# Graph attention with neighbour rows gathered for whole tiles: blocks of edges aligned to tiles instead of to groups of four tiles

## The reference

```python
Wh = x @ W_w + W_b
e = (Wh @ a_w[:256])[col] + (Wh @ a_w[256:])[row] + a_b[0]     # row = src, col = dst
e = where(e > 0, e, 0.2 * e)
m = segment_max(e, row)
ex = exp(e - m[row])
att = ex / segment_sum(ex, row)[row]
h = relu(segment_sum(att[:, None] * Wh[col], row))             # one row of 256 per edge is fetched
```

## Time and profile before

| what | us |
|---|---|
| median of three runs | 2610.23 (2609.86 to 2613.34) |
| profiled execution, its own time | 2611.51 |
| span of its trace | 2609.7 |
| first gather to last `gather_up` begins | 739.0 to 2081.7 |
| busy in the span: PE, PEld | 2045.7, 1599.1 |
| busy in the span: DVE, ACT, POOL | 1908.9, 1587.7, 1356.0 |

### The profile page before, as it was taken

The page is one execution under the profiler, slowest core; times in us unless marked ns, Lnnn a source line. Parts: engine busy times, 40 slices in busy tenths (PEclk is TensorE's granted clock), DMA queues, the critical chain, the costliest instruction groups (busy, mean ns, idle before and its releaser), DMA issues. The chain is left out here.

```text
span 2609.7 us, 49796 instructions
## 1 busy us (share of the span) xinstructions
PE 2045.7 (78%) x10254; PEld 1599.1 (61%) x10254; DVE 1908.9 (73%) x6660; ACT 1587.7 (61%) x4949; POOL 1356.0 (52%) x1284
## 2 busy tenths in 40 slices
PE   2888766788738788888888888888888766099997
PEld 1444355677636666666666666666766556088886
DVE  7877689999857878878888887788888664045453
ACT  4566375333137778878887788778877764033332
POOL 0000000011257777777777777777777447645555
PEclk9999968899869989999999899989989866599999
DMA  4100000111133433333333333333333265435553
GB/s 147 40 27 27 19 10 19 50 24 24 21 83 106 111 106 106 107 106 108 106 106 108 109 105 107 107 108 107 106 107 105 64 180 131 116 69 92 96 93 59
DMA packets 130120, 223.27 MB, mean 86 GB/s; under 512 B 37607, under 2 KB 80660, under 8 KB 129820
## 3 DMA queue, kind: packets, MB, share of 16 engines
q0 software_dynamic: 78864, 160.18, 25.3%
q1 hardware_dynamic: 49418, 58.93, 7.6%
q10 hardware_dynamic: 1538, 1.31, 0.2%
HBM read 171.72 MB, written 49.77 MB: 85 GB/s over the span
## 5 line engine op out<-in xcount | busy, mean ns | idle before, releaser
L1213 POOL DMA_INDIRECT area<-wh_table,area x1004 | 1010.9, 1007 | 319.4 <-issue 299.4
L1453 PE MATMUL bank<-area 128*126 128x258 f32 x2008 | 563.9, 429 | 48.5 <-ACT area L1398 39.1
L1453 PEld LDWEIGHTS bank<-area 128*126 128x126 f32 x2008 | 399.4, 209 | 155.1 <-ACT area L1398 86.7
L512 POOL DMA_INDIRECT sorted_slots<-area x28 | 45.7, 1633 | 672.2 <-issue 486.3
L1398 ACT ACTIVATE area<-area 128x126 f32<-128x126 f32 x1004 | 317.5, 388 | 97.5 <-issue 84.4
L1242 DVE TENSOR_SCALAR area<-iota_row,area 128x126 f32<-128x126 f32 x1004 | 358.7, 361 | 21.1 <-issue 7.5
L1389 ACT ACTIVATE area<-iota_row,area 128x126 f32<-128x126 f32 x1004 | 315.9, 388 | 0.0
L1435 PE MATMUL bank<-ident,area 128*126 128x128 f32 x1004 | 168.4, 294 | 115.6 <-DVE area L1242 114.5
L1943 POOL DMA_INDIRECT out_dram<-area x108 | 169.9, 1573 | 160.3 <-DVE area L2002 143.5
L1435 PEld LDWEIGHTS bank<-ident,area 128*126 128x126 f32 x1004 | 122.6, 147 | 163.1 <-DVE area L1242 129.3
L1472 PE MATMUL bank<-area 128*128 128x250 f32 x800 | 201.1, 395 | 0.0
(11 more groups left out here) (340 smaller groups left out, 4281.0 us busy)
## 6 DMA issues: line engine op xcount, KB each, us to landing
area<-wh_table,area POOLq DMA_INDIRECT x1004
area<-moe_rows SPq DMA_DIRECT2D x54, 264.0 KB, 2.7
wh_table<-area SPq DMA_DIRECT2D x50, 126.0 KB
xn<-in_x_dram SPq DMA_DIRECT2D x25, 250.0 KB
x_rows<-area SPq DMA_DIRECT2D x25, 250.0 KB
area<-x_rows SPq DMA_DIRECT2D x25, 250.0 KB
area<-in_L_ffn_expert_w_dram SPq DMA_DIRECT2D x3, 1536.0 KB, 12.0
out_dram<-xn SPq DMA_DIRECT2D x2, 1500.0 KB
```

Of the source, the lines that this page charges most:

```text
L1213: g.indirect_dma_start(out=gath[:, s % RG, t, :], out_offset=None, in_=table, in_offset=bass.IndirectOffsetOnAxis(ap=idx_tab[:, s * GT + t ...
L1453: last = T.matmul(bank[US][0:RW, 0:WROW], sm[:, b, t, :], gath[:, j % RG, t, :], start=(t == 0), stop=(t == GT - 1))
```

## The change

A node block's edges now begin at a whole tile, not at a whole group. There are TILES = 860 tiles (215 ring blocks of four). NG is still 251: each node block is still cut into groups of four tiles from its own first tile, and the last group of a block reaches into the next block's tiles. The slots of a foreign tile must not count, so `row_tab` now holds row + 2^17 x block, and `shifted` subtracts 2^17 x (the group's block), which gives `rowl`; slots of another block match no row. The 60.0 bound on the exponent (`score_bound`) goes, and the distance factor becomes 1e12.

The gathered tiles lie in a ring of 40 tile places (RS), in the order of tiles. A group's first tile (`tile_tab`), its place in the ring (`slot_tab`), how many tiles it needs (`group_tab` row 0), where its new scores go (`group_tab` row 32) and its block (row 64) are tables in SBUF which the engines load into registers, group by group. SP hands on two counts: `room` to POOL when a ring block has been used up (it loads the group number from `group_tab` row 96 and waits for `p_main` against it), and `ready` to DVE when a ring block has landed.

`own` becomes `own_all` for every block, filled with the row score parts once, so the copy in `group_peak` goes. ACT's `divide` writes the maximum's parts there and loads the block's register. The `x1` reload moves from SP's queue to ACT's. The first stage gains the instructions that make the tables.

```diff
-GS, GS_BITS = GT * L, 9
-NG = (E + NT * (LO - 1 + GS - 1)) // GS
-TILES = NG * GT
+MOST = (E + NT * (LO - 1 + L - 1)) // L
+NG = (MOST + NT * (GT - 1)) // GT
+NB = -(-(MOST + GT - 1) // GT)
+TILES = NB * GT
...
+                for b in range(NB):
+                    f = b + AHEAD
+                    if RING <= f < NB:
+                        sp.reg_load(uses[f % 2], group_tab[96:97, f - RING:f - RING + 1])
+                        sp.wait_ge(p_main, sp.snap(uses[f % 2], min_val=1, max_val=NG))
+                        sp.sem_inc(room, 1)
+                    sp.wait_ge(gathered[b % RING], 16 * GT * (b // RING + 1))
+                    sp.sem_inc(ready, GT)
...
-                for s in range(NG):
-                    if s >= RG:
-                        g.wait_ge(p_main, s - RG + 1)
-                    for t in range(GT):
-                        g.indirect_dma_start(out=gath[:, s % RG, t, :], out_offset=None, in_=table,
+                for b in range(NB):
+                    if b >= RING:
+                        g.wait_ge(room, b - RING + 1)
+                    for i in range(GT * b, GT * b + GT):
+                        g.indirect_dma_start(out=gath[:, (i + GT) % RS, :], out_offset=None, in_=table,
...
                 def shifted(s, j):
-                    b = j % 2
-                    dve.wait_ge(gathered[j % RG], at((s[0], 2 * PER // RG, j // RG), 16 * GT, 16 * GT))
+                    dve.reg_load(needs[j % 2], group_tab[0:1, bass.ds(at(s), 1)])
+                    dve.reg_load(puts[j % 2], group_tab[32:33, bass.ds(at(s), 1)])
+                    dve.reg_load(blocks[j % 10], group_tab[64:65, bass.ds(at(s), 1)])
+                    dve.reg_load(wins[j % 5], slot_tab[0:1, bass.ds(at(s), 1)])
+                    dve.reg_load(firsts[j % 2], tile_tab[0:1, bass.ds(at(s), 1)])
+                    first = dve.snap(firsts[j % 2], min_val=0, max_val=TILES - GT)
+                    put = dve.snap(puts[j % 2], min_val=0, max_val=RS - GT)
+                    wait(dve, a_dist, at(s, 1, -4))
+                    V.tensor_scalar(rowl[:, j % 5, :], row_tab[:, bass.ds(first, GT)], iota_blk[:, bass.ds(block_of(j), 1)], None, ALU.subtract)
+                    dve.wait_ge(ready, dve.snap(needs[j % 2], min_val=GT, max_val=TILES))
+                    wait(dve, d_x, at(s))
+                    wait(dve, d_es, at(s, 3, -13))
                     wait(dve, p_xt, at(s, 1, -1))
-                    V.tensor_scalar(fdc[:, b, :], gath[:, j % RG, :, D], shift[:, :], None, ALU.add).then_inc(d_fdc, 1)
+                    V.tensor_tensor(fdr[:, :, :, bass.ds(put, GT)],
+                                    gath[:, bass.ds(put, GT), D].unsqueeze(1).unsqueeze(1).to_broadcast([128, 2, 2, GT]),
+                                    lift2.unsqueeze(2).unsqueeze(3).to_broadcast([128, 2, 2, GT]), ALU.add).then_inc(d_fdc, 1)
...
-                    dve.reg_load(blocks[j % 4], group_block[0:1, bass.ds(at(s), 1)])
-                    r = block_of(j)
-                    wait(dve, p_q, at(s, 1, -1))
-                    hold(dve)
-                    V.tensor_copy(own[0:R, b, 0:3], fr_parts[:, bass.ds(r, 1), :].rearrange("p a k -> p (a k)"))
...
-                    V.tensor_scalar(e4[:, b, :], e3[:, b, :], 60.0, None, ALU.min).then_inc(d_e, 1)
...
+                    act.reg_load(blocks[b], group_tab[64:65, bass.ds(at(s), 1)])
...
+                def load_places(s, j):
+                    for t in range(GT):
+                        pe.reg_load(places[j % 2][t], slot_tab[32 * t:32 * t + 1, bass.ds(at(s), 1)])
+
+                def load_block(s, j):
+                    pe.reg_load(blocks[j % 2], group_tab[64:65, bass.ds(at(s), 1)])
...
-                        last = T.matmul(bank[US][0:RW, 0:WROW], sm[:, b, t, :], gath[:, j % RG, t, :], start=(t == 0), stop=(t == GT - 1))
+                        place = pe.snap(places[b][t], min_val=0, max_val=RS - 1)
+                        last = T.matmul(bank[US][0:RW, 0:WROW], sm[:, b, t, :], gath[:, bass.ds(place, 1), :].rearrange("p a w -> p (a w)"),
+                                        start=(t == 0), stop=(t == GT - 1))
...
-                together(pe, [(5, total), (3, fetch)], feed, [(0, turn)])
+                together(pe, [(5, total), (3, fetch)], feed, [(0, turn), (4, load_places), (2, load_block)])
```

More of the change, by code:

```diff
@@ L325, in gps_kernel @@
         vrow = take(TILES).bitcast(I32)
+        tcmp, iota_t = take(TILES)[0:NT, :], take(TILES)[0:NT, :]
+        tf = take(NG)
+        spot, whole, over = take(2 * NG), take(2 * NG), take(2 * NG)
+        turns = take(2 * NG).bitcast(I32)
+        ti32 = take(NG).bitcast(I32)
+        rcmp = take(2, NB)
         XB, QB, HEADS, NUM, DEN, OUT = 0, 1, 2, 3, 4, 5
@@ L1145, in _ @@
                 pe.wait_ge(staged, KC)
+                for i in range(-(-TILES // 512)):
+                    a, b = 512 * i, min(TILES, 512 * i + 512)
+                    T.matmul(bank[i][:, 0:b - a], ones[0:NT, :], tcmp[:, a:b], start=True, stop=True)
                 pe.wait_ge(slots_in, 16 * -(-TILES // 128))
@@ L1159, in gps_kernel @@
         sm = take(2, GT, RW)
-        fdc = take(2, GT)
+        fdr = take(2, 2, RS)
+        fdr_all = fdr.rearrange("p k d n -> p k (d n)")
+        rowl = take(5, GT)
+        lift2 = take(2)
         gmax, gt, gl = take(2), take(2), take(2)
@@ L1163, in gps_kernel @@
         alpha = take(5)
-        own = take(6).bitcast(BF16).rearrange("p (b k) -> p b k", b=2)
         new, left = take(2), take(2)
@@ L1167, in gps_kernel @@
         mrun = take(NT)
-        e1, e2, e3, e4 = (take(2, GT) for _ in range(4))
+        e1, e2, e3 = (take(2, GT) for _ in range(3))
         XT, QE, US = (0, 3), 1, 2
@@ L1173, in gps_kernel @@
         x1_in = [sem(f"x1_in{i}") for i in range(2)]
-        gathered = [sem(f"gathered{i}") for i in range(RG)]
+        gathered = [sem(f"gathered{i}") for i in range(RING)]
+        room = sem("room")
+        ready = sem("ready")
         d_fdc = sem("d_fdc")
@@ L1192, in _ @@
             def _(sp):
-                def load_x1(c, j):
-                    wait(sp, m_ln[1], at(c, 4, -7))
-                    sp.dma_start(x1[0:R, j, :, :].rearrange("p t d -> p (t d)"), x1_rows[bass.ds(at(c, R), R), :]).then_inc(x1_in[j], 16)
-                def feed(slot, c, j, now):
-                    following = now and not (isinstance(c[0], int) and at(c) + 1 >= NC)
-                    if slot == 5 and following:
-                        load_x1((c[0], 2, c[2] + 1), 1 - j)
-                load_x1((0, 2, 0), 0)
-                together(sp, feed)
+                sp.dma_start(x1[0:R, 0, :, :].rearrange("p t d -> p (t d)"), x1_rows[0:R, :]).then_inc(x1_in[0], 16)
+                uses = [sp.alloc_register(f"uses{i}") for i in range(2)]
+                for b in range(NB):
[6 more added lines that the diff above has]
+                    sp.sem_inc(ready, GT)
             @block.gpsimd
```

185 lines of the change are left out of this document (129 added, 56 removed).

## The result

The changed kernel takes **3114.05 us** (median of four runs, 3111.88 to 3117.55); the kernel before, on the same chip, 2611.78 (2609.86 to 2613.97). The ratio is 1.192, 95% interval 1.190 to 1.194. I had forecast 2905 with a range from 2800 to 3060: the direction was right, the size was not, and the time lies outside the range. The profiled execution of after spans 3111.5 us.

A forecast was written before the change was run, and what follows sets the result against it. POOL's gathers were taken to bound the kernel, with DVE 0.32 us a step behind. 2611.5 + 284 (longer DVE step, net of the gathers' gain) + 10 (first stage) = 2905.5, stated as 2905 us; range 2800 to 3060.

The forecast's parts named there:

- The bound and the gathers: Second stage: POOL's gathers set 5.23 us a step, DVE next at 4.91; 144 fewer gathers are worth only 80 us.
- The marks in the profile: Signs expected in the new trace: POOL waiting for `room`, hardly any DVE gather waits, 1.3 to 1.5 us idle before `rowl`.
- Setup: First stage: about 38 more small DVE instructions for the tables, on the path, 10 us more.
- Register loads on DVE, 2.05 us for five: Five loads a group instead of one, behind `group_peak`: 2.05 us at 0.41 each, bounds 1.25 and 2.5.
- Between the loads and the sum, 6 x 0.1 + 0.13: DVE step after the loads: six register instructions and waits at 0.1 us, then 0.13 from `shifted` to the sum.
- From the sum to `gather_up`, 2.86 to 2.66: Rest of the DVE step: 34 listed instructions become 32, so 0.2 us less.
- The mean step, 6.36: DVE's mean step, feed-forward steps included: 4.91 + 1.44, taken as 6.36 us; against 5.23, +284 us.
- Register loads on PE, nothing: Five loads a group between `turn` and `total`, covered by PE's wait for DVE's marks: no charge.
- ACT, SP and POOL, nothing: ACT's one load a group, SP's `ready` and `room`, and POOL's waits for room: no charge.
- The rival that makes PE the bound: PE's loads find no cover, plain steps take 6.1 us instead of 5.5: +105, 3010 us, chance 0.15.
- Loads overlap: Rival: DVE's sequencer does not stop for loads, five cost 0.95 + 0.3 us: 2701 us, chance 0.11.
- the gain stays: Rival: DVE's sequencer has unseen cover, added work counts nothing, 80 us go and 10 come: 2540 us, chance 0.06.

The follow-up runs named there:

- b_gather860: The kernel before with 144 of its 1004 gathers left out (860 remain, stale rows in the buffer), nothing else changed: 2532.2 us, ratio 0.970.
- b_loads5: The kernel before with four more register loads a step on DVE, all from the same entry at partition 0, gathers unchanged: 2793.98 us, ratio 1.070.
- a_one_side: a0_clamp with DVE's block number loaded from partition 32 instead of 64, so none of its five loads leaves the lower half: 3016.9 us, ratio 1.155.
- a_pe_early: a0_clamp with TensorE's five register loads of a step put ahead of its transposes instead of behind them: 3126.03 us, ratio 1.194.
- a_pe_loads8: a0_clamp with three more register loads a step on TensorE, for separate copies of the block number: 3197.25 us, ratio 1.224.
- a_packed: a0_clamp with DVE's five values of a group packed in one word, loaded once and unpacked by register instructions: 2789.72 us, ratio 1.068.
- a0_clamp: The changed kernel with one more register instruction a step on DVE and one per ring block on SP, limiting awaited counts: 3128.59 us, ratio 1.198.
- b_alu10: The kernel before with ten more register instructions a step on DVE, between the block number's load and its use: 2669.58 us, ratio 1.022.

## Why the prediction was right in direction and wrong in size

**The bound and the gathers: right.** POOL was the bound by 0.32 us a step, and DVE stood behind it. The term of 80 us is 80.5 (b_gather860). The marks in the profile came in kind: POOL waits for `room`, DVE hardly for rows, an idle without releaser stands ahead of `rowl`. They did not come in size: the idle is 1.84 us where 1.3 to 1.5 were named, two of the loads start 0.64 us apart where 0.4 was named, the plain step is 6.47 for 5.5 and the mean 7.18 for 6.4. But b_loads5 shows that the 80 us are no gain of the change as it stands: with a step over 5.23 us they come with 1004 gathers too.

**Setup: right.** 10 us forecast, 10.7 measured (up to 14.7 in the other traces with tiles).

**Register loads on DVE, 2.05 us for five: the step that failed first.** From the first load's index instruction, 1505.83, to the end of the last load, 1508.38, it is 2.55 us, which was my upper bound. I took the price of all five from one pair at line 1993, and both loads of that pair read partition 0. The table's rows lie at partitions 0, 32 and 64, and the list `needs, puts, blocks, wins, firsts` crosses over and back. Of the difference of 0.50 us, 0.45 is the crossing, two loads of 0.53 instead of 0.30; without it the forecast's 0.41 a load stands. In a_one_side it was worth 112 us. None of the rows that I had read of before shows two loads in different halves. But I had the upper bound, 2.5, and my range used it with every other term held at its middle.

**Between the loads and the sum, 6 x 0.1 + 0.13: too small.** From the last load's end to `shifted` (1508.38 to 1509.19) it is 0.81 instead of 0.6. I had counted six register instructions and waits and put `rowl` under them. In the trace seven stand there, and `rowl` takes a place of its own in the queue behind the second: eight places of 0.1.

**From the sum to `gather_up`, 2.86 to 2.66: wrong in sign.** Measured 2.95. I counted two instructions less at 0.1 each. What `score_bound` left did come back: it stood between the third mark and the fourth, which now starts 0.46 us behind the third for 0.63. But the index of the score window is computed behind the wait for the reduce: L1382 to L1385 is 0.34 us, L1295 to L1298 before 0.21; and the third mark starts 0.61 behind the second for 0.54. A count does not tell which instructions stand behind a wait. The three differences, 0.50, 0.21 and 0.29, are 1.00 us; 6.47 - 5.50 is 0.97. So the mechanism was right and its size was not: the full sequencer was charged 1.44 us a step, and it took 2.27 (7.18 - 4.91).

**The mean step, 6.36: measured 7.18.** The steps with feed-forward work grew a little less than the plain ones, and in about every second plain step the queue stands 0.35 us longer (6.82 for 6.47), where before that was about every fifth. 7.18 - 6.36 = 0.82, x 251 = 206, and the miss is 3114 - 2905 = 209.

**The ledger by runs**, from 2532.2 up: four more loads 262 (b_loads5), two changes of half 112 (a_one_side; 104 by its step), setup 11; that makes 2917. The other 197 us of the 3114 are 0.78 us a step. The trace of plain steps has about as much: some 0.37 for a computed address in front of each of the four added loads (their starts are 0.41 to 0.44 apart, a change of half left out, where b_loads5 has 0.335), 0.38 between the last load and `shifted` (0.81 against 0.43 in b_loads5), 0.07 net behind it. This last part is read from traces and not taken apart by a run. The third rival of the experiments, `rowl`, the wait on `ready` and the wider `shifted`, lies in those 0.38 us. Of the wait itself the trace shows 2.3 us in all; what the rest would be without `rowl` was not tried.

**Register loads on PE, nothing: right, by a small margin** (a_pe_early, a_pe_loads8). The rival that makes PE the bound showed only where DVE's step had been shortened (`gather_up` waits 20.0 us for `total` in a_one_side, 69.0 in a_packed) or PE's lengthened (68.7 in a_pe_loads8). The granted clock of TensorE did fall, from 0.92 in the second stage before (850 to 2050 us) to 0.86 (850 to 2450 us), and a product of `total` takes 476 ns on average instead of 429; since PE had room to spare, that shows nowhere in the time. **ACT, SP and POOL, nothing: right.** DVE waited 2.3 us for SP.

**The rivals.** *Loads overlap* (2701) is refuted by b_loads5, and *the gain stays* (2540) with it: there is cover, but 0.30 us of it, where the loads alone need 1.34, and in a0_clamp it is used up and one register instruction more shows. On the price of a load, the Trainium skill, page "DMA: Bandwidth & Descriptors", section "Latency and other measured facts", gives about 600 ns at least for a `tensor_load` and says that unrolling by four amortizes it. By an estimate from the Trainium skill's 600 ns the four loads of b_loads5 would have been 602 us over 2532, 3134; it was at 2794. The runs decide against the figure: they show 0.30 us on DVE and 0.53 after a change of half. They show no amortization either, as loads in a row start 0.335 us apart.

## What to carry to other kernels

Where engine instructions are short, count what the sequencer does, not the busy shares: DVE's engine was busy 973 of 1200 us in the second stage before, when POOL set the pace and DVE stood 0.32 us a step behind, and 958 of 1600 after, when DVE's queue set it. Values that a loop reads into registers belong in one word, or at least in one half of the partitions, and in the order that crosses least; packing five loads into one gave back 339 us here. And before relieving an engine, ask what the next bound leaves of it: here 0.32 us a step, less than one register load with its address.

## What the runs showed of the hardware

- A register load lasts 0.30 us on DVE and on PE when the engine's load before it read the same half of the partitions (0 and 32, or 64 and 96), and 0.52 to 0.53 on DVE, 0.48 to 0.49 on PE, after one from the other half. The halves are told from these four starting partitions; 64 next to 96 was seen on PE alone. The section of loads pays it in full (0.48 us less for two in a_one_side), the step 0.415 of it, since another engine came next.
- Loads of independent registers on one queue run one after the other, 0.335 us apart with the same address, 0.41 to 0.44 with a new one.
- Register instructions in a row start 0.074 us apart on DVE's queue. In the step one cost 0.055 us on average over ten, with some cover (b_alu10), and 0.044 without (a0_clamp, where the trace shows it merged with the MOVE next to it, into one FUSED_REGOPS of 92 ns).
- DVE's queue stood 0.35 us longer at regular places: in after at 1517.24, 1545.06, 1560.81 and 1576.44 us, between instructions whose starts are 0.44 to 0.46 us apart there and 0.07 to 0.10 elsewhere. Counted in DVE's records these places are 256, 128 and 128 instructions apart. What stops it was not tried. In plain steps such a stop falls on 73 of 155 in after and on 28 of 155 in before, with more instructions a step in after.
